# Attention and router stage of a gated block: who turns the attention outputs to token rows, and who normalises

## The chip, the cores and the metric

One core of a Trainium2 chip. The time is device microseconds of one execution; three runs of the kernel before gave 2321.11 us as their median (2320.79 to 2324.24). Inputs and outputs are float32.

## What is computed

```python
# x: (64, 128, 512), ctx: (64, 128, 128); 32 query heads on 8 key/value heads, head size 16
def xattn(q, k, v):
    scores = einsum('bkgsd,bktd->bkgst', qh, kh) / sqrt(16)
    weights = softmax(scores, axis=-1)
    return einsum('bkgst,bktd->bkgsd', weights, vh)      # back to (B, S, 512)

x = x + tanh(g_xattn) * xattn(layernorm(x), ctx, ctx)
h = layernorm(x)                                          # 8192 rows of 512
probs = softmax(h @ Wr)                                   # 32 experts, top 4, renormalised
shared = (silu(h @ Wsg) * (h @ Wsu)) @ Wsd * sigmoid(h @ Wse)
# each expert takes its first 64 (row, choice) pairs through silu(.Wg) * (.Wu) @ Wd
x = x + tanh(g_ffn) * (shared + weighted expert outputs)
```

## The kernel before

The program has two stages. The first is the attention stage, one loop over the 64 batches of 128 rows; it also adds the residual, computes the second normalisation and the router's logits, and picks the top four experts. The second stage runs the shared and the routed experts, in tiles of 512 rows; the change does not touch it. Everything below is about the first stage.

Each engine runs its own hand-written program, and the engines meet only at semaphores. `iterations` calls `body(B)` for B = 0 to 67, the middle ones in a hardware loop of two bodies a turn. So the order of an engine's work is the order of its `body`, and the work is pipelined by hand: in one body an engine works on several batches. A body has four chunks, c = 0 to 3. In the notation of the code, b = B - 2 means that the step is for the batch two before.

What TensorE does in a body, by name and line: p_exp, the scores of batch B - 1 (L663), one chunk each; in every chunk four transpositions of the next query chunk into p_tq (`q_cols`, L622) and the score maxima of batch B into p_max (L711); `k_cols` of batch B + 1 in chunk 3 (L614), into the bank p_pv; `pv`, the product of the exponentials with the values, in chunk 0 for (B - 2, half 1) and in chunk 2 for (B - 1, half 0) (L638), into p_pv; `o_cols`, which turns the evacuated product to token rows in p_ot (L648), in chunks 1 and 3; the transposition of the normalised x of B - 3 in chunk 1 (L673), into p_pv; the router's logits of B - 4 in chunk 2 (L686), into p_ot; and p_mt, the transposed maxima, in chunks 0 and 2 (L699). p_max, p_tq, p_pv, p_ot and p_mt each have one buffer: the next user waits until the last one has been read.

VectorE reduces p_max in every chunk (L561), normalises x for the queries (`norm_x`, L504), takes the statistics of x (L489, `bn_stats`, and L495), inverts the sums and normalises the outputs out of p_ot (L517, L527), adds the residual (L540), takes the statistics of the sum, normalises it (L504 again, target xn), and runs the router's selection (L546 copy of the logits, L573, L580, L585, L597). ScalarE does the exponentials (L439), and evacuates p_tq (L423), p_pv (L416, L417 for the keys, L428 for the outputs, L452 for the transposed x) and p_mt (L446). GpSimd splits keys and queries into their stacks (L339 to L342, L358, L362), computes one over the deviation (`inverse_root`, L327 and L331), books the selection (`take_top`) and splits a part of the shared weights (L400). SP issues the DMAs.

`pv` puts four groups into four quarters of p_pv's partitions, 512 columns each (four heads by 128 rows), so that what is evacuated has head dimensions on the partitions and has to be turned:

```python
for q in range(4):
    g = 4 * s + q
    last = mm(p_pv[32 * q:32 * q + 32, :], vals[b.par][:, g, :],
              probs[2 * s + q // 2][:, 512 * (q % 2):512 * (q % 2) + 512], start=True, stop=True)
```

Of the kernel before, what the change touches and what calls it, by code (L numbers as in the profile page):

```python
# [98 lines left out]
def build(nc, x, ctx_in, g_xattn, g_ffn, Wr, Wg, Wu, Wd, Wsg, Wsu, Wsd, Wse, out):  # L99
# [7 lines left out]
    with stack:  # L107
# [29 lines left out]
        with ExitStack() as scope:  # L137
# [11 lines left out]
            ot_sb = [sb(f"ot_sb{i}", [128, 512]) for i in range(2)]  # L149
# [19 lines left out]
            is_top = [sb(f"is_top{i}", [128, TOPK, NE]) for i in range(2)]  # L169
            two_sum = sb("two_sum", [128, 2, NE])  # L170
# [32 lines left out]
            pv_mm, ot_mm, mt_mm = sem("pv_mm"), sem("ot_mm"), sem("mt_mm")  # L203
# [36 lines left out]
            def _(sp):  # L240
# [12 lines left out]
                def body(B):  # L253
# [4 lines left out]
                    for c in range(NC):  # L258
# [6 lines left out]
                        if c == 0:  # L265
# [41 lines left out]
            def _(pool):  # L307
# [15 lines left out]
                def inverse_root(b, stat, mv, ve, rs, used, done):  # L323
# [7 lines left out]
                    nc.gpsimd.tensor_tensor(rs[:, :], ve[:, :], mhalf[:, :], ALU.pow).then_inc(done, 1)  # L331
# [50 lines left out]
                def body(B):  # L382
                    if isinstance(B.n, int) and B.n == 0:
                        inverse_root(B, stat1, mv1, ve1, rs1, qraw_done, rs1_done)
                        k_stacks(B)
                        q_stacks(B)
                        inverse_root(B + 1, stat1, mv1, ve1, rs1, qraw_done, rs1_done)
# [3 lines left out]
                    if (B - 5).ok:  # L391
                        take_top(B - 5)
                    if (B + 2).ok:
                        inverse_root(B + 2, stat1, mv1, ve1, rs1, qraw_done, rs1_done)
                    if (B - 2).ok:
                        inverse_root(B - 2, stat2, mv2, ve2, rs2, xn_done, rs2_done)
# [823 lines left out]
```

## Time and profile before

| | |
|---|---|
| median of 3 runs | 2321.11 us |
| the profiled execution, its own time | 2320.78 us |
| its span, first to last instruction | 2319.0 us |
| mean granted TensorE clock | 0.996 of full speed |
| TensorE busy | 2281.3 us (98%) |
| VectorE busy | 1154.4 us (50%) |
| ScalarE busy | 763.7 us (33%) |
| GpSimd busy | 594.0 us (26%) |
| DMA | 235.11 MB, mean 101 GB/s |

The shares are over the whole span, and the two stages differ: in the first, up to about 727 us, four engines work side by side; in the second TensorE leads. In what follows PE is TensorE's matmul stream, PEld its weight loads, which may run ahead of the matmuls, DVE is VectorE, ACT is ScalarE, POOL is GpSimd. A busy PE says little by itself, because the ends of pipelined matmuls are modelled; how far apart the groups start says more.

### The profile page before, as it was taken

How to read it: one execution, taken by the hardware profiler on the slowest of the kernel's cores; microseconds unless marked ns; L12 is line 12 of the kernel's file. 1: busy time of each engine (PE TensorE's matmuls, PEld its weight loads, DVE VectorE, ACT ScalarE, POOL GpSimd, SP SyncE). 2: the span in 40 equal slices, each digit the busy share in tenths (PEclk: the TensorE clock that was granted, in tenths of full speed). 3: DMA queues.
4: the chain of work that ended last, by engine and by line, in shares of the span. 5: the costliest groups of instructions: out<-in, count | busy, mean ns of one | idle time of the engine just before them, and what ended most of it. 6: DMA issues, size and time to landing. Idle time of an engine off the chain costs nothing.

```text
span 2319.0 us, 40286 instructions
## 1 busy us (share of the span) xinstructions
PE 2281.3 (98%) x12417; PEld 1760.4 (76%) x12417; DVE 1154.4 (50%) x2218; ACT 763.7 (33%) x1312; POOL 594.0 (26%) x1395
## 2 busy tenths in 40 slices
PE   6999999999997999999999999999999999999999
PEld 4777777777776877777777777778777777777777
DVE  6999999999996733222232322233232332323232
ACT  5888888888884111010100101011010110101010
POOL 5677777777763100000000000000000000000100
PEclk9999999999998999999999999999999999999999
DMA  3555555555554132322122222222222123222421
GB/s 85 142 142 145 144 144 141 145 145 144 138 153 137 19 119 88 114 84 81 63 79 84 97 86 82 79 68 97 99 84 79 63 81 119 81 83 75 137 67 43
DMA packets 269453, 235.11 MB, mean 101 GB/s; under 512 B 120545, under 2 KB 196321, under 8 KB 269410
## 3 DMA queue, kind: packets, MB, share of 16 engines
q1 hardware_dynamic: 265058, 221.89, 31.9%
q0 software_dynamic: 4352, 12.65, 1.9%
q8 instruction: 26, 0.43, 0.1%
q14 instruction: 17, 0.14, 0.0%
HBM read 161.88 MB, written 71.57 MB: 101 GB/s over the span
## 4 chain that ended last, share of the span: by engine, by line
PE 67%; DVE 1%; DMA 0%; issue 0%; DVEq 0%; POOLq 0%
PE acc L1126 7%; PE p_u L1142 7%; PE p_u L1144 7%; PE p_u L1143 7%; PE acc L1128 7%; PE acc L1127 7%; PE p_g L1142 7%; PE p_g L1144 7%; PE p_g L1143 7%; PE p_x L1174 2%; PE p_y L1161 2%; PE p_x L1161 2%; PE p_x L1152 0%; DMA rows<-out_dram 0%; PE p_y L1167 0%; DVE rows L1106 0%
## 5 line engine op out<-in xcount | busy, mean ns | idle before, releaser
L1060 DVE TENSOR_TENSOR act_f<-p_u,act_f 128x512 f32<-128x512 f32 x176 | 121.8, 692 | 982.7 <-PE p_u L1144 982.6
L965 ACT ACTIVATE act_f<-p_g 128x512 f32<-128x512 f32 x176 | 105.3, 598 | 1215.8 <-PE p_g L1144 1194.8
L561 DVE TENSOR_REDUCE negmax<-p_max 128x8 f32<-128x1024 f32 x256 | 312.8, 1222 | 49.6 <-PE p_max L711 47.8
L1126 PE MATMUL acc<-wd_h,hh 128*128 128x512 f32 x704 | 279.5, 397 | 0.0
L1142 PE MATMUL p_u<-xh,wgu_h 128*128 128x512 f32 x704 | 274.1, 389 | 4.0 <-DVE act_f L1060 4.0
L1142 PE MATMUL p_g<-xh,wgu_h 128*128 128x512 f32 x704 | 275.6, 391 | 0.0
L1127 PE MATMUL acc<-wd_l,hh 128*128 128x512 f32 x704 | 274.3, 390 | 0.0
L1128 PE MATMUL acc<-wd_h,hl 128*128 128x512 f32 x704 | 274.3, 390 | 0.0
L1144 PE MATMUL p_g<-xh,wgu_l 128*128 128x512 f32 x704 | 274.0, 389 | 0.0
L1144 PE MATMUL p_u<-xh,wgu_l 128*128 128x512 f32 x704 | 273.9, 389 | 0.0
L1143 PE MATMUL p_u<-xl,wgu_h 128*128 128x512 f32 x704 | 273.9, 389 | 0.0
L1143 PE MATMUL p_g<-xl,wgu_h 128*128 128x512 f32 x704 | 273.9, 389 | 0.0
L439 ACT ACTIVATE probs<-p_exp 128x1024 f32<-128x1024 f32 x256 | 261.2, 1020 | 31.8 <-PE p_exp L663 27.8
L711 PE MATMUL p_max<-kt,qt 128*128 128x256 f32 x1024 | 185.2, 303 | 1.5 <-DVE negmax L561 1.4
L1126 PEld LDWEIGHTS acc<-wd_h,hh 128*128 128x128 f32 x704 | 132.1, 188 | 47.6 <-DVE hl L1066 13.0
L663 PE MATMUL p_exp<-qt,kt 128*128 128x512 f32 x512 | 163.5, 401 | 0.2
L922 POOL DMA_INDIRECT eo<-out_dram,cur_tok x32 | 31.2, 976 | 505.0 <-DMA out_dram<-rows 408.3
L622 PE MATMUL p_tq<-ident,qs 128*128 128x128 f32 x1024 | 155.8, 275 | 2.6 <-POOL qs L362 1.8
L1142 PEld LDWEIGHTS p_u<-xh,wgu_h 128*128 128x128 f32 x704 | 132.2, 188 | 32.3 <-DVE act_f L1060 4.9
L1128 PEld LDWEIGHTS acc<-wd_h,hl 128*128 128x128 f32 x704 | 132.2, 188 | 28.0
L1144 PEld LDWEIGHTS p_g<-xh,wgu_l 128*128 128x128 f32 x704 | 132.2, 188 | 27.6
L1144 PEld LDWEIGHTS p_u<-xh,wgu_l 128*128 128x128 f32 x704 | 132.2, 188 | 27.4
(142 smaller groups left out, 3545.2 us busy)
## 6 DMA issues: line engine op xcount, KB each, us to landing
ew<-in_L_ffn_Wg_dram SPq DMA_DIRECT2D x32, 704.0 KB, 6.0
ew<-in_L_ffn_Wu_dram SPq DMA_DIRECT2D x32, 704.0 KB, 7.4
xs<-in_x_dram SPq DMA_DIRECT2D x64, 256.0 KB, 2.6
xres<-in_x_dram SPq DMA_DIRECT2D x64, 256.0 KB, 2.9
out_dram<-x SPq DMA_DIRECT2D x64, 256.0 KB, 2.7
xn_rows<-xn SPq DMA_DIRECT2D x64, 256.0 KB, 3.0
xn_cols<-xnT SPq DMA_DIRECT2D x64, 256.0 KB, 3.3
rows<-out_dram SPq DMA_DIRECT2D x16, 1024.0 KB, 5.2
```

The source lines that it names most:

```text
L439: nc.scalar.activation(probs[c][:, :], p_exp[:, :, :].rearrange("p a b -> p (a b)"), ACT.Exp, scale=float(D) ** -0.5).then_inc(exp_done, 1)
L561: nc.vector.tensor_reduce(negmax[c // 2][:, :].rearrange("p (g c i) -> p c i g", g=2, c=2)[:, c % 2, :, :], p_max[:, :, :].rearrange("p a ...
L622: last = tr(p_tq[:, 128 * i:128 * i + 128], qs[b.par][:, c, i, :, :].rearrange("p g r -> p (g r)"), ident[:, :])
L663: last = mm(p_exp[:, g2, :], kt[b.par][:, c, 128 * g2:128 * g2 + 128], qt[b.par][:, c, :], start=True, stop=True)
L711: last = mm(p_max[:, i // 2, 256 * (i % 2):256 * (i % 2) + 256], qt[B.par][:, c, 128 * i:128 * i + 128], kt[B.par][:, c, :], start=True, s ...
L1060: nc.vector.tensor_tensor(act_f[:, :], p_u[:, :], act_f[:, :], ALU.mult).then_inc(h_done, 1)
L1126: mm(acc[:, j, :], a[:, t], wd_h[:, f, :], start=(f == 0), stop=False)
L1127: mm(acc[:, j, :], a[:, t], wd_l[:, f, :], start=False, stop=False)
L1128: last = mm(acc[:, j, :], b[:, t], wd_h[:, f, :], start=False, stop=(f == FC - 1))
L1142: mm(bank[:, :], wgu_h[:, w, k, cols], xh[:, k, :], start=(k == 0), stop=False)
L1143: mm(bank[:, :], wgu_h[:, w, k, cols], xl[:, k, :], start=False, stop=False)
L1144: last = mm(bank[:, :], wgu_l[:, w, k, cols], xh[:, k, :], start=False, stop=(k == KC - 1))
```

## The change

- `pv` writes the product in 16 pieces, one for each of four groups of heads and four blocks of 32 rows: the 32 rows' block chooses the partition quarter, the group the columns. Each piece has 128 columns (four heads by 32 rows).
- With this layout a transposition of 32x32 blocks gives token rows. VectorE does it, out of p_pv into SBUF (`turn`, tile `turned`). TensorE's `o_cols` and ScalarE's `pv_evac` are gone. Reciprocal and normalisation of the outputs read `turned`.
- Both normalisations go from VectorE to ScalarE, as one Identity with scale and bias; GpSimd's `inverse_root` computes the bias nm = -mean * rs besides, with one more instruction.
- xn's transposition goes into p_ot. The logits go to chunk 3, their copy to ScalarE, and the selection follows one batch later (B - 5, `take_top` B - 6).
- SP stores xn at the end of the body.

```diff
@@ SP @@
-                            if (B - 3).ok:
-                                b = B - 3
-                                wait(sp, xn_done, b.n + 1)
-                                sp.dma_start(xn_dram[bass.ts(b.n, 128), 0:E], xn[b.par][:, :]).then_inc(xn_out[b.par], 16)
...
+                    if (B - 3).ok:
+                        b = B - 3
+                        wait(sp, xn_done, b.n + 1)
+                        sp.dma_start(xn_dram[bass.ts(b.n, 128), 0:E], xn[b.par][:, :]).then_inc(xn_out[b.par], 16)
@@ GpSimd, inverse_root @@
-                    nc.gpsimd.tensor_tensor(rs[:, :], ve[:, :], mhalf[:, :], ALU.pow).then_inc(done, 1)
+                    chain.inc(nc.gpsimd.tensor_tensor(rs[:, :], ve[:, :], mhalf[:, :], ALU.pow))
+                    chain.wait(pool)
+                    alone(pool, spare_p)
+                    nc.gpsimd.tensor_scalar(nm[:, :], mv[b.par][:, 0:1], rs[:, 0:1], -1.0, ALU.mult, ALU.mult).then_inc(done, 1)
@@ ScalarE @@
-                def pv_evac(b, s):
-                    act.wait_ge(pv_mm, 2 * b.n + s + 1)
-                    wait(act, ot_mm, 2 * (b.n - 1) + s + 1)
-                    nc.scalar.activation(ot_sb[s][:, :], p_pv[:, :], ACT.Copy).then_inc(pv_done, 1)
+                def norm_x(b):
+                    act.wait_ge(rs1_done, b.n + 1)
+                    wait(act, qs_done, b.n - 1)
+                    nc.scalar.activation(qraw[b.par][:, :], xs[b.par][:, :], ACT.Identity, bias=nm1[:, 0:1], scale=rs1[:, 0:1]).then_inc(qraw_done, 1)
+
+                def norm_x2(b):
+                    act.wait_ge(rs2_done, b.n + 1)
+                    wait(act, xnT_mm, b.n - 1)
+                    wait(act, xn_out[b.par], 16 * b.half)
+                    nc.scalar.activation(xn[b.par][:, :], x2[b.par][:, :], ACT.Identity, bias=nm2[:, 0:1], scale=rs2[:, 0:1]).then_inc(xn_done, 1)
...
+                        if c == 0 and (B + 1).ok:
+                            norm_x(B + 1)
...
-                        if c == 0 and (B - 2).ok:
-                            pv_evac(B - 2, 1)
-                        if c == 2 and (B - 1).ok:
-                            pv_evac(B - 1, 0)
+                        if c == 0 and (B - 3).ok:
+                            norm_x2(B - 3)
...
+                        if c == 3 and (B - 4).ok:
+                            b = B - 4
+                            act.wait_ge(lg_mm, b.n + 1)
+                            wait(act, kept, b.n - 1)
+                            nc.scalar.activation(lg[b.par][:, :], p_ot[:, 0:NE + 1], ACT.Copy).then_inc(lg_done, 1)
@@ VectorE @@
+                def turn(b, s):
+
+                    dve.wait_ge(pv_mm, 2 * b.n + s + 1)
+                    wait(dve, ot_done, 2 * (b.n - 1) + s + 1)
+                    nc.vector.transpose(turned[s][:, :, :].rearrange("p n r -> p (n r)"), p_pv[:, :]).then_inc(pv_done, 1)
@@ TensorE @@
                     for q in range(4):
-                        g = 4 * s + q
-                        last = mm(p_pv[32 * q:32 * q + 32, :], vals[b.par][:, g, :],
-                                  probs[2 * s + q // 2][:, 512 * (q % 2):512 * (q % 2) + 512], start=True, stop=True)
+                        heads = probs[2 * s + q // 2][:, 512 * (q % 2):512 * (q % 2) + 512].rearrange("p (i s) -> p i s", i=G)
+                        for j in range(4):
+                            last = mm(p_pv[32 * j:32 * j + 32, 128 * q:128 * q + 128], vals[b.par][:, 4 * s + q, :],
+                                      heads[:, :, 32 * j:32 * j + 32], start=True, stop=True)
                     last.then_inc(pv_mm, 1)
-
-                def o_cols(b, s):
-                    pe.wait_ge(pv_done, 2 * b.n + s + 1)
...
```

What waits for the bank p_pv keeps its line in `k_cols`: `wait(pe, pv_done, 2 * b.n - 3)`, for batch B + 1 the count that was reached by the evacuation of (B - 1, half 0) and is now reached by its `turn`.

The rest of the change is the order. TensorE before, chunks 2 and 3 of one body (p_tq<-ident,qs are q_cols, p_pv<-ident,ks k_cols, p_ot<-wr,xnT the logits):

```order
L663 MATMUL p_exp<-qt,kt 128x512 x2
L638 MATMUL p_pv<-probs,vals 32x512 x4
L686 MATMUL p_ot<-wr,xnT 128x33 x4
L699 MATMUL p_mt<-ident,negmax 16x128
L622 MATMUL p_tq<-ident,qs 128x128 x4
L711 MATMUL p_max<-kt,qt 128x256 x4
L663 MATMUL p_exp<-qt,kt 128x512 x2
L614 MATMUL p_pv<-ident,ks 128x128 x4
L648 MATMUL p_ot<-ident,ot_sb 128x128 x4
L622 MATMUL p_tq<-ident,qs 128x128 x4
L711 MATMUL p_max<-kt,qt 128x256 x4
```

The same place of the change:

```order
L676 MATMUL p_exp<-qt,kt 128x512 x2
L660 MATMUL p_pv<-probs,vals 32x128 x16
L707 MATMUL p_mt<-ident,negmax 16x128
L645 MATMUL p_tq<-ident,qs 128x128 x4
L719 MATMUL p_max<-kt,qt 128x256 x4
L676 MATMUL p_exp<-qt,kt 128x512 x2
L637 MATMUL p_pv<-ident,ks 128x128 x4
L698 MATMUL p_ot<-wr,xnT 128x33 x4
L645 MATMUL p_tq<-ident,qs 128x128 x4
L719 MATMUL p_max<-kt,qt 128x256 x4
```

The logits have moved from behind PV to behind k_cols, and o_cols is gone from there.

VectorE before, from the reduction of chunk 1 to that of chunk 3:

```order
L561 TENSOR_REDUCE negmax<-p_max 128x4x2
L540 SCALAR_TENSOR_TENSOR x_0<-o_sb,tanh_x,xres 128x512
L546 COPY lg<-p_ot 128x33
L489 BN_STATS st<-x_0 128x6
L561 TENSOR_REDUCE negmax<-p_max 128x4x2
L573 MAX v_0<-lg 128x8
L495 BN_AGGR mv_0<-st 128x2
L580 MAX_INDEX i<-v_0,lg 128x8
L561 TENSOR_REDUCE negmax<-p_max 128x4x2
```

The same place of the change, with what follows to the end of the body:

```order
L610 TENSOR_REDUCE negmax<-p_max 128x4x2
L594 SCALAR_TENSOR_TENSOR x_0<-o_sb,tanh_x,xres 128x512
L506 BN_STATS st<-x_0 128x6
L523 STREAM_TRANSPOSE turned<-p_pv 128x512
L561 CAST idx_f<-i 128x4
L512 BN_AGGR mv_0<-st 128x2
L610 TENSOR_REDUCE negmax<-p_max 128x4x2
L568 TENSOR_TENSOR is_top<-iota_e,idx_f 128x128
L610 TENSOR_REDUCE negmax<-p_max 128x4x2
L529 RECIPROCAL rec<-turned 128x16
L539 TENSOR_TENSOR o_sb<-turned,rec 128x256
```

The turn of (B - 1, half 0) stands between the statistics of x2 and the reduction of chunk 2, the selection's cast and the aggregation have moved ahead of that reduction. In chunk 0 the turn of (B - 2, half 1) stands ahead of the reduction, and the statistics of x, max8, reciprocal, aggregation, max_index and normalise stand between the reductions of chunks 0 and 1.

## Rows read from the trace of the kernel before

**Rows 1.** Busy time by engine (--windows), 400 to 700 us; first row names the columns.

```profile
core 0: us, PE busy (x) PEld busy (x) DVE busy (x) ACT busy (x) POOL busy (x), PEclk, DMA share, GB/s
400.00:700.00 300.00, 299.30 (x2282) 219.59 (x2281) 280.31 (x581) 254.37 (x431) 210.78 (x537) 1.00 0.54 146
```

**Rows 2.** Groups of instructions in 400:700: busy us, mean ns, then idle us before.

```profile
L561 DVE TENSOR_REDUCE negmax<-p_max 128x8 f32<-128x1024 f32 x112 | 136.9, 1222 | 15.5 <-PE p_max L711 14.6
...
L504 DVE TENSOR_SCALAR xn<-x,mv,rs 128x512 f32<-128x512 f32 x28 | 21.6, 770 | 0.0
...
L504 DVE TENSOR_SCALAR qraw<-xs,mv,rs 128x512 f32<-128x512 f32 x27 | 14.5, 536 | 0.0
...
L546 DVE COPY lg<-p_ot 128x33 f32<-128x33 f32 x27 | 4.9, 181 | 0.9 <-PE p_ot L686 0.9
```

**Rows 3.** Timeline of VectorE, one batch: start us, us, instruction, idle before.

```profile
502.83 0.68 DVE L489 BATCH_NORM_STATS2 st<-xs 128x6 f32<-128x512 f32 x1
...
503.43 0.23 DVE L517 RECIPROCAL rec<-p_ot 128x16 f32<-128x16 f32 x1
503.66 0.18 DVE L495 BATCH_NORM_AGGREGATE mv<-st 128x2 f32<-128x6 f32 x1
...
503.77 0.42 DVE L527 TENSOR_TENSOR o_sb<-p_ot,rec 128x256 f32<-128x256 f32 x1
...
504.11 1.22 DVE L561 TENSOR_REDUCE negmax<-p_max 128x8 f32<-128x1024 f32 x1
...
505.24 0.90 DVE L540 SCALAR_TENSOR_TENSOR x<-o_sb,tanh_x,xres 128x512 f32<-128x512 f32 x1
...
506.18 0.69 DVE L489 BATCH_NORM_STATS2 st<-x 128x6 f32<-128x512 f32 x1
...
508.07 0.18 DVE L573 MAX8 v<-lg 128x8 f32<-128x32 f32 x1
...
508.18 0.17 DVE L495 BATCH_NORM_AGGREGATE mv<-st 128x2 f32<-128x6 f32 x1
...
508.48 0.18 DVE L580 FIND_INDEX8 i<-v,lg 128x8 uint32<-128x32 f32 x1
...
509.10 1.23 DVE L561 TENSOR_REDUCE negmax<-p_max 128x8 f32<-128x1024 f32 x1 [0.43 <-PE p_max L711]
...
514.77 1.22 DVE L561 TENSOR_REDUCE negmax<-p_max 128x8 f32<-128x1024 f32 x1
```

**Rows 4.** Timeline of VectorE, the reduction of chunk 1 sixteen batches later.

```profile
676.63 1.22 DVE L561 TENSOR_REDUCE negmax<-p_max 128x8 f32<-128x1024 f32 x1
```

**Rows 5.** Timeline of TensorE and of ScalarE's evacuation, the same batch.

```profile
500.49 0.57 ACT L428 ACTIVATE ot_sb<-p_pv 128x512 f32<-128x512 f32 x1
...
501.25 0.42 PEld L673 LDWEIGHTS p_pv<-ident,xn 128*128 128x128 f32 x4 [0.33 <-ACT ot_sb L428]
...
503.71 0.16 PEld L638 LDWEIGHTS p_pv<-probs,vals 128*32 128x32 f32 x8 [0.36 <-issue]
503.71 1.07 PE L638 MATMUL p_pv<-probs,vals 128*32 128x512 f32 x8
...
504.71 1.08 PE L686 MATMUL p_ot<-wr,xnT 128*128 128x33 f32 x8
...
505.62 0.27 PE L699 MATMUL p_mt<-ident,negmax 128*16 128x128 f32 x1
...
507.11 0.60 PE L614 MATMUL p_pv<-ident,ks 128*128 128x128 f32 x4
...
507.55 0.60 PE L648 MATMUL p_ot<-ident,ot_sb 128*128 128x128 f32 x4
...
507.88 0.47 PEld L622 LDWEIGHTS p_tq<-ident,qs 128*128 128x128 f32 x4
```

**Rows 6.** Groups of instructions, whole span: 512 elements out of PSUM, and ScalarE out of SBUF.

```profile
L1060 DVE TENSOR_TENSOR act_f<-p_u,act_f 128x512 f32<-128x512 f32 x176 | 121.8, 692 | 982.7 <-PE p_u L1144 982.6
...
L946 ACT ACTIVATE xh<-chosen 128x512 fp32r<-128x512 f32 x60 | 33.0, 621 | 32.7 <-PE p_u L1144 32.7
```

More of the change, by code:

```diff
@@ L148, in build @@
             probs = [sb(f"probs{i}", [128, 2 * 512]) for i in range(4)]
-            ot_sb = [sb(f"ot_sb{i}", [128, 512]) for i in range(2)]
+            turned = [sb(f"turned{i}", [128, 16, 32]) for i in range(2)]
             o_sb = sb("o_sb", [128, E])
@@ L451, in body @@
                             wait(act, lg_mm, b.n - 1)
[L452 to L456 removed]
+                            nc.scalar.activation(xnT[b.par][:, :, :].rearrange("p k t -> p (k t)"), p_ot[:, :], ACT.Copy).then_inc(xnT_done, 1)
+                        if c == 0 and (B - 3).ok:
+                            norm_x2(B - 3)
                         if c == 3 and (B + 1).ok:
@@ L531, in body @@
                         aggregate(B, st1, stats_x(B), mv1, stat1)
-                        norm_x(B)
                         aggregate(B + 1, st1, stats_x(B + 1), mv1, stat1)
                     for c in range(NC):
+                        if c == 0 and (B - 2).ok:
+                            turn(B - 2, 1)
+                        if c == 1:
+                            if (B - 2).ok:
+                                inverted = invert_sums(B - 2, 1)
+                            if (B + 2).ok:
+                                wait(dve, rs1_done, B.n + 1)
+                                aggregate(B + 2, st1, x_stats, mv1, stat1)
+                            if (B - 5).ok:
+                                top_count = top_places(B - 5, top_count)
+                            if (B - 2).ok:
+                                normalise(B - 2, 1, inverted)
                         if c == 2 and (B - 2).ok:
@@ L575, in body @@
[L575 to L586 removed]
+                            if (B - 5).ok:
+                                top_count = top_eight(B - 5)
@@ L669, in body @@
                             pe.wait_ge(xn_done, b.n + 1)
-                            pe.wait_ge(pv_done, 2 * b.n + (4 if (b + 1).ok else 2))
-                            wait(pe, xnT_done, b.n)
+                            wait(pe, lg_done, b.n - 1)
                             for k in range(KC):
-                                last = tr(p_pv[:, 128 * k:128 * k + 128], xn[b.par][:, 128 * k:128 * k + 128], ident[:, :])
+                                last = tr(p_ot[:, 128 * k:128 * k + 128], xn[b.par][:, 128 * k:128 * k + 128], ident[:, :])
                             last.then_inc(xnT_mm, 1)
@@ L678, in body @@
                             pv(B - 1, 0)
-                        if c == 2 and (B - 4).ok:
+                        if c == 3 and (B - 4).ok:
                             b = B - 4
-                            pe.wait_ge(xnT_done, b.n + 1)
-                            pe.wait_ge(ot_done, 2 * b.n + 6 if (b + 2).ok else 2 * NB)
-                            wait(pe, lg_done, b.n)
+                            pe.wait_ge(xnT_done, b.n + (2 if (b + 1).ok else 1))
+                            if not (b + 1).ok:
+                                pe.wait_ge(lg_done, b.n)
                             for k in range(KC):
@@ L689, in body @@
                             pv(B - 2, 1)
-                        if c == 1 and (B - 2).ok:
-                            o_cols(B - 2, 1)
-                        if c == 3 and (B - 1).ok:
-                            o_cols(B - 1, 0)
                         b, h = (B - 1, 1) if c == 0 else (B, 0)
```

130 lines of the change are left out of this document (54 added, 76 removed).

## The prediction

> **What bounds the kernel now.** I read the windows first. In 400 to 700 us, inside the attention loop, TensorE is busy 299.3 of 300 us, VectorE 280.3, ScalarE 254.4, GpSimd 210.8 [rows 1]. The same reduction L561, 16 batches apart, starts at 504.11 and 676.63 [rows 3, 4]: 10.78 us a batch. The batch that I read closely takes 10.66 (its neighbour, with the loop's branch, some 0.2 more). Per batch that is VectorE 10.0 us, ScalarE 9.0, GpSimd 7.5. TensorE and VectorE are both nearly without gaps: in the timeline VectorE's instructions follow each other from 502.83 to 508.6, and its only real idle time is 0.43 us ahead of the reduction at 509.10 [rows 3]. So an average tells little; what counts is the order in which the two engines hand p_max and p_pv to each other. All that the change touches lies in this loop (up to about 727 us); the expert stage behind it is the same code.
>
> **Terms.**
>
> *TensorE loses o_cols.* Four transpositions take 0.44 us (7.11 to 7.55 in rows 5), eight of them 0.88 us a batch. The xn transposition moves from p_pv to p_ot and costs the same; the logits move from chunk 2 to chunk 3, 0.91 us either way [rows 5].
>
> *PV is cut into 16 products of 128 columns.* Before, eight passes of 512 columns, four side by side, take 1.07 us, and the next group starts 1.00 us after the first [rows 5]. The columns streamed are the same. Lower bound: the same 1.00 us. Upper bound: nothing runs side by side, 32 passes at the 0.11 us of a transposition, 3.5 us. I take 1.0 to 1.2, because the four neighbours still write four different partition quarters, as now, and their eight weight loads are issued within 0.16 us [rows 5].
> The Trainium skill ("TensorE: Matmul & The Clock Gate", Part 1) gives a floor of about 25 ns between starts of matmuls, or 62 ns where the sequencer decodes them. By the first, 32 passes would be 0.8 us and change nothing; by the second 2.0 us. The row above shows eight loads far closer together than either, but only as a burst.
>
> *VectorE.* Gone are norm_x (0.54), norm_x2 (0.77) and the lg copy (0.18) [rows 2]. New are two block transpositions of 128x512 from PSUM. No row shows one. Nearest is L1060, 512 elements from PSUM in 0.69 us [rows 6]. Lower bound 0.54, a 512-element instruction of the cheapest kind (norm_x); upper bound 1.22, as if it went over the data twice (the 1,024-element reduction). I take 0.69. Reciprocal and normalise now read SBUF; they cost what they cost now or up to 0.06 less each. Net: -1.49 + 1.38, less 0 to 0.24. VectorE's load stays within 0.4 us of the 10.0.
>
> *ScalarE* swaps two evacuations for two normalisations (a 512-column ACTIVATE out of SBUF is 0.62, L946 [rows 6]; the evacuation at 500.49 is 0.57 [rows 5]) and gets the lg copy: 9.0 to about 9.4 us, below the period. *GpSimd* gets two small instructions a batch with a wait ahead of each, under 1 us on 7.5. Its wait for qraw gets shorter, since ScalarE normalises ahead of the first exp and not behind VectorE's reduction. *SP:* the store of xn goes behind the loads and the out store of its batch; its reader comes two batches later, so nothing. If ScalarE or GpSimd were late, k_stacks or qraw would be late next; both have over half a batch.
>
> *Where the turn now stands.* This is the term that decides. p_pv has one bank, and three users in turn: PV, k_cols, and (before) xn. k_cols of the next batch waits in chunk 3 for the bank to be read. Before, ScalarE read it right after PV. Now VectorE's turn(B-1, 0) must, and it stands behind the reduction of chunk 1, x2 and the statistics of x2 (the order rows above show it). Behind k_cols on TensorE now stand the logits, q_cols and p_max of chunk 3, for whose reduction VectorE then waits. Following that loop from reduction 1 to reduction 1, start to start:
> - reduction 1.13 (4.11 to 5.24); x2 0.84 mean and 0.04 until statistics may start, 0.88; statistics 0.60 (2.83 to 3.43) [rows 3];
> - turn 0.69, and 0.19 until TensorE's first weight load (ACT L428 ends at 501.06, PEld L673 starts 501.25 [rows 5]); so far 3.49;
> - k_cols 0.44, logits 0.91, q_cols and p_max until the reduction starts 1.22 (weight load 507.88 to 509.10) [rows 3, 5]; 6.06;
> - reduction 3 in full 1.22 and 0.19; p_mt 0.11; q_cols and p_max 1.22; 8.80;
> - reduction 0 1.13, statistics 0.60, max8 0.11, reciprocal 0.23, aggregate 0.11, max_index 0.20, normalise 0.34 [rows 3]; 11.52.
>
> **11.5 us against the 10.66 of the same batch**, while either engine alone would need about 10. On the path are therefore the turn and the logits; off it are o_cols, PV (0.2 us of room in chunk 0) and all of ScalarE's. I take +0.8 a batch on 58 full batches (of 64, less the first and last that lack the router or the output step): +46 us. The end of the loop gets one router step later and two longer links (nm, ScalarE's norm): +2. The profiled execution took 2320.8 us (span 2319.0), 0.3 below the median, which changes nothing: **2369 us**.
>
> Its own range: turn at 0.54 and the four small instructions 0.06 cheaper give 11.1, +24, 2345; turn at 1.22 gives 12.05, +78, 2399.
>
> **Rivals.**
>
> *A. The work decides, and it gets faster.* If the turn came early enough, TensorE would need 10.66 - 0.88 + 0 to 0.2 = 9.8 to 10.0 and VectorE 9.6 to 9.9; at 10.0 the loop saves 0.7 x 60 = 42: 2279. For it speaks that both engines run nearly gapless now, so the loops they form have found room. It decides from the point where turn(B-1, 0) ends before TensorE is through p_exp of chunk 3, that is some 0.5 us earlier, and the rest of the loop is also 0.4 shorter. Against it: the order is written out and VectorE is strictly in order, and even without the wait of k_cols the path by reduction 2 is 1.13 + 0.88 + 0.60 + 0.61 + 0.18 + 1.41 + 0.79 = 5.60 instead of 6.06, 11.06 in all. This is the other sign.
> The Trainium skill ("VectorE: DVE Perf Modes", The three transpose paths) has a 128x128 bf16 transposition at 311 ns on VectorE against 390 on TensorE and calls VectorE's the fastest within a 32x32 block; by that rule the move gains. No row here shows that form, and the loop above is against it: TensorE's cost is 0.11 us each in a stream, not its latency.
>
> *B. No change.* It needs the loop at 10.7: nothing that I can name gives 0.8 back except sums of small errors (releases faster than 0.19, twice; cheaper small instructions). 2321.
>
> *C. The block transposition takes twice,* 1.22: 2399, or a little over.
>
> *D. PV costs more.* Between the bounds, at 2.0 us (32 passes at a bit over half the pace of a transposition [rows 5], side by side in part only), 0.2 of the extra 1.0 is covered in chunk 0, so +0.8 more a batch: 2415. At 3.5 us TensorE alone needs about 15 a batch: some 2580. For it: the passes are four times as many, and a quarter as long. Against it: they stay in four quarters.
>
> **Numbers.** Forecast 0.60; A 0.15; B 0.04; C 0.10; D 0.08 and 0.02 in its extreme; 0.01 for a faster case in between. Slower: 0.80; same 0.04; faster 0.16 (over or under 0.2%, about 5 us, is what a measurement of this kernel can tell from no change). Range 2335 to 2400: my own case, its cheap end with 10 us of doubt on the count, and most of C. Left out are A, B and D.
>
> **What would show it.** In the profile after: a STREAM_TRANSPOSE of about 0.7 us; L561's fellow at 11.4 to 11.6 us a batch; weight loads of k_cols (p_pv<-ident,ks) that wait 0.4 to 0.7 us for VectorE's turn in each batch; the p_max of chunk 3 later than now, with VectorE idle 0.5 us ahead of its reduction; TensorE's busy share in 400:700 near 90%. PV's 32 passes near 1.1 us. A turn over 1 us makes it C; PV over 1.5 us D. I am wrong if k_cols does not wait, or if the period is under 10.8 with all that in place.

## The result, and the profile after

The changed kernel takes **2347.77 us** (median of 4 runs, 2346.22 to 2349.66) beside 2321.92 (2320.79 to 2324.24) of the kernel before: a ratio of 1.011, 95% interval 1.0093 to 1.0128. It is slower by 26 us. I had said 2369 and 2335 to 2400: right in direction and inside the range, and about twice too much. The profiled execution has a span of 2347.8 us against 2319.0.

Windows of the changed kernel, 400 to 700 us, to set beside [rows 1]:

```profile
core 0: us, PE busy (x) PEld busy (x) DVE busy (x) ACT busy (x) POOL busy (x), PEclk, DMA share, GB/s
400.00:700.00 300.00, 275.11 (x3248) 219.66 (x3248) 264.76 (x533) 259.85 (x442) 222.71 (x569) 1.00 0.51 137
```

TensorE and VectorE both got gaps: 299.3 has become 275.1, 280.3 has become 264.8. Per batch VectorE's busy time went from 10.07 us (280.3 x 10.78 / 300) to 9.92 (264.8 x 11.24 / 300) and TensorE's from 10.75 to 10.31. The work fell on both, and the loop still got longer. Groups of VectorE and ScalarE in the same stretch, beside [rows 2]:

```profile
L610 DVE TENSOR_REDUCE negmax<-p_max 128x8 f32<-128x1024 f32 x108 | 131.2, 1214 | 32.4 <-PE p_max L719 32.1
L523 DVE STREAM_TRANSPOSE turned<-p_pv 128x512 f32<-128x512 f32 x54 | 37.8, 701 | 0.0
L539 DVE TENSOR_TENSOR o_sb<-turned,rec 128x256 f32<-128x256 f32 x53 | 27.4, 517 | 0.9
...
L433 ACT ACTIVATE qraw<-xs,nm,rs 128x512 f32<-128x512 f32 x27 | 22.0, 814 | 0.0
L439 ACT ACTIVATE xn<-x,nm,rs 128x512 f32<-128x512 f32 x27 | 21.6, 799 | 0.0
```

The turn is 0.70 us. VectorE now waits 32.1 us in 300 for p_max, where it waited 14.6. The list of waits (engine and line, what it waited for: us in total, times, longest) has what I looked for first:

```profile
DVE negmax L610 <- PE p_max L719: 32.1, 40, 1.1
...
PEld p_pv L637 <- DVE turned L523: 19.1, 27, 0.8
```

In each of the 27 batches the weight loads of k_cols wait 0.7 us for VectorE's turn. One round of VectorE, from reduction 1 to reduction 1, and the same reduction 16 batches later (timeline: start, us, instruction, idle before):

```profile
500.24 1.21 DVE L610 TENSOR_REDUCE negmax<-p_max 128x8 f32<-128x1024 f32 x1
501.37 0.75 DVE L594 SCALAR_TENSOR_TENSOR x<-o_sb,tanh_x,xres 128x512 f32<-128x512 f32 x1
502.15 0.69 DVE L506 BATCH_NORM_STATS2 st<-x 128x6 f32<-128x512 f32 x1
502.76 0.70 DVE L523 STREAM_TRANSPOSE turned<-p_pv 128x512 f32<-128x512 f32 x1
...
503.51 1.19 DVE L610 TENSOR_REDUCE negmax<-p_max 128x8 f32<-128x1024 f32 x1
...
505.97 1.23 DVE L610 TENSOR_REDUCE negmax<-p_max 128x8 f32<-128x1024 f32 x1 [1.07 <-PE p_max L719]
...
508.71 1.23 DVE L610 TENSOR_REDUCE negmax<-p_max 128x8 f32<-128x1024 f32 x1 [0.25 <-PE p_max L719]
...
511.42 1.22 DVE L610 TENSOR_REDUCE negmax<-p_max 128x8 f32<-128x1024 f32 x1
...
680.11 1.21 DVE L610 TENSOR_REDUCE negmax<-p_max 128x8 f32<-128x1024 f32 x1
```

(680.11 - 500.24) / 16 = 11.24 us a batch; before it was 10.78 [rows 3, 4]. 0.46 x 60 = 27 us, all of the loss. The last reduction of the loop starts at 703.2 before and at 730.7 after, 27.5 later. From there to the end it is 1615.8 us before and 1617.1 after, so the experts' stage costs what it did to within the spread of the runs.

The most useful table is that of the steps from each reduction to the next (start to start, us, from the timelines; each batch has one of each):

| | 0 to 1 | 1 to 2 | 2 to 3 | 3 to 0 | batch, mean of 48 |
|---|---|---|---|---|---|
| before, one body | 2.87 | 2.81 | 2.16 | 2.80 | 10.78 |
| before, mean | 2.86 | 2.84 | 2.16 | 2.91 | 10.78 |
| after, one body | 2.71 | 3.27 | 2.46 | 2.74 | 11.24 |
| after, mean | 2.77 | 3.27 | 2.46 | 2.74 | 11.24 |

(The loop has two bodies; the other one is up to 0.25 longer in one step. Steps given below are of one body unless they are called means.) Before, VectorE has at most 0.17 us of gap ahead of its reductions in 3 to 0, 0 to 1 and 1 to 2, and only 2 to 3 is a hand-over by way of TensorE. In the means, the change took 0.17 out of 3 to 0 and 0.09 out of 0 to 1, and it put the turn into 1 to 2, which was already full and grew by 0.43; from there the turn pushes k_cols, and 2 to 3 grew by 0.29.

The same batch on TensorE:

```profile
503.51 0.42 PEld L637 LDWEIGHTS p_pv<-ident,ks 128*128 128x128 f32 x4 [0.66 <-DVE turned L523]
...
503.90 0.97 PEld L698 LDWEIGHTS p_ot<-wr,xnT 128*128 128x128 f32 x8
...
504.71 0.50 PEld L645 LDWEIGHTS p_tq<-ident,qs 128*128 128x128 f32 x4
...
506.33 0.81 PEld L660 LDWEIGHTS p_pv<-probs,vals 128*32 128x32 f32 x32 [0.36 <-issue]
...
507.34 0.09 PEld L707 LDWEIGHTS p_mt<-ident,negmax 128*16 128x16 f32 x1 [0.20 <-issue]
```

The turn ends at 503.46 and k_cols starts at 503.51; the logits and Q follow without a gap. PV in 32 passes takes 1.01 us to the next group, as it did in 8.

### The profile page after: what moved, and what is told of

Its sections match the earlier page's. It is cut to its first block, busy times and chain, and to the rows that moved or that the text cites. A ratio compares the mean times of both kernels' runs of the same rounds, so it can differ in the third digit from the quotient of the medians.

```text
span 2347.8 us, 45660 instructions
## 1 busy us (share of the span) xinstructions
PE 2255.0 (96%) x14977; PEld 1783.5 (76%) x14977; DVE 1141.5 (49%) x2154; ACT 802.1 (34%) x1376; POOL 637.0 (27%) x1523
## 4 chain that ended last, share of the span: by engine, by line
PE 66%; DVE 1%; DMA 0%; issue 0%; DVEq 0%; POOLq 0%
PE acc L1134 7%; PE p_u L1150 7%; PE p_u L1152 7%; PE p_u L1151 7%; PE acc L1135 7%; PE acc L1136 7%; PE p_g L1150 7%; PE p_g L1152 7%; PE p_g L1151 7%; PE p_x L1182 2%; PE p_y L1169 2%; PE p_x L1169 2%; PE p_x L1160 0%; DMA rows<-out_dram 0%; PE p_y L1175 0%; DVE rows L1114 0%
## 5 line engine op out<-in xcount | busy, mean ns | idle before, releaser
L453 ACT ACTIVATE probs<-p_exp 128x1024 f32<-128x1024 f32 x256 | 261.4, 1021 | 32.8 <-PE p_exp L676 32.1
L645 PE MATMUL p_tq<-ident,qs 128*128 128x128 f32 x1024 | 162.8, 282 | 2.6 <-POOL qs L366 1.9
L428 ACT ACTIVATE qt<-p_tq 128x512 fp32r<-128x512 f32 x256 | 150.7, 589 | 19.6 <-PE p_tq L645 12.1
```

The lines of the kernel that those rows point to most:

```text
L428: nc.scalar.activation(qt[b.par][:, c, :], p_tq[:, :], ACT.Copy).then_inc(tq_done, 1)
L453: nc.scalar.activation(probs[c][:, :], p_exp[:, :, :].rearrange("p a b -> p (a b)"), ACT.Exp, scale=float(D) ** -0.5).then_inc(exp_done, 1)
L645: last = tr(p_tq[:, 128 * i:128 * i + 128], qs[b.par][:, c, i, :, :].rearrange("p g r -> p (g r)"), ident[:, :])
```

## Experiments

Twelve kernels ran. Each is an edit of the changed kernel, unless it says otherwise; the ratio is to the kernel before, run beside it. "Batch" is the mean of the same 48 batches.

### e1_turn_before_stats

```diff
-                            dve.wait_ge(x2_done, b.n + 1)
-                            x2_stats = stats(x2[b.par][:, :], st2)
                         if c == 2 and (B - 1).ok:
                             turn(B - 1, 0)
+                        if c == 2 and (B - 2).ok:
+                            dve.wait_ge(x2_done, (B - 2).n + 1)
+                            x2_stats = stats(x2[(B - 2).par][:, :], st2)
```

> The change with one edit: VectorE's turn of (B - 1, half 0) ahead of the statistics of x2, not behind them. Theory (the turn's place): in the change the turn ends at 503.46 and k_cols starts at 503.51, 0.61 after p_exp of chunk 3 is through (about 502.90); then logits, q_cols and p_max stand behind it. Now the turn starts 0.61 earlier, k_cols no longer waits for it, q_cols ends at 504.57, and p_max of chunk 3 starts when reduction 2 ends (504.70), 0.43 earlier than now (505.18): 10.8 us a batch for 11.24, so 0.43 x 60 = 26 us less, 2322 us. Rival 1 (chunk 2 of VectorE is too full, whatever the turn's place: reduction 2 is what p_max of chunk 3 waits for): no change, 2348, since reduction 2 starts no earlier. Rival 2 (ScalarE's normalisations, at 0.80 us each and not 0.62, are on the path): no change, 2348.

Measured: 2339.06 (2337.49 to 2342.14), ratio 1.0078, 1.0061 to 1.0095; batch 11.09. Steps 2.71, 3.42, 2.12, 2.7 to 2.9. Timeline of VectorE:

```profile
505.33 1.22 DVE L611 TENSOR_REDUCE negmax<-p_max 128x8 f32<-128x1024 f32 x1
506.47 0.74 DVE L594 SCALAR_TENSOR_TENSOR x<-o_sb,tanh_x,xres 128x512 f32<-128x512 f32 x1
507.13 0.71 DVE L523 STREAM_TRANSPOSE turned<-p_pv 128x512 f32<-128x512 f32 x1
507.76 0.65 DVE L506 BATCH_NORM_STATS2 st<-x 128x6 f32<-128x512 f32 x1
508.33 0.15 DVE L561 CAST idx_f<-i 128x4 f32<-128x4 uint32 x1
508.56 0.18 DVE L512 BATCH_NORM_AGGREGATE mv<-st 128x2 f32<-128x6 f32 x1
508.75 1.23 DVE L611 TENSOR_REDUCE negmax<-p_max 128x8 f32<-128x1024 f32 x1
...
510.87 1.23 DVE L611 TENSOR_REDUCE negmax<-p_max 128x8 f32<-128x1024 f32 x1 [0.69 <-PE p_max L720]
```

The half that my theory is about came true: k_cols waits no longer (0.05 us where it was 0.71), and 2 to 3 falls from 2.46 to 2.12, a bare hand-over. But 1 to 2 grew by 0.15, and the whole gave 9 us of the 26 that I had expected. The turn no longer covers the time between the statistics and their aggregation: the aggregation starts 0.80 us after the statistics do, where the turn used to stand between them and only 0.04 us lay between the cast and the aggregation. The chunk is full of VectorE's own work in either order. Of the 0.46 us a batch that the change lost, the reordering gives back 0.15; the other 0.31 is still lost with k_cols free of the turn.

### e2_logits_chunk2

```diff
-                        if c == 3 and (B - 4).ok:
+                        if c == 2 and (B - 4).ok:
```

(TensorE's logits, back to where they stood before.)

> The change with one edit: TensorE's logits back in chunk 2, behind PV, as before the change. Theory: the turn still ends at 503.46, and k_cols waits for it; behind k_cols only q_cols is left (0.47), so p_max of chunk 3 comes at about 504.92 instead of 505.18 (reduction 2, itself 0.15 later because of the logits in chunk 2, ends at 504.87): 0.27 a batch, 16 us, 2332 us. Rival 1 (VectorE's chunk 2 decides): slower or the same, 2348 to 2357, as reduction 2 only comes later. Rival 2 (ScalarE): the same.

Measured: 2348.07 (2347.99 to 2349.66), ratio 1.0115, 1.0098 to 1.0131; batch 11.20. Steps 2.71, 3.4 to 3.6, 2.12, 2.85. A miss: 2 to 3 shrank by 0.34, and k_cols no longer waits for the turn (0.05 us), but in the means 1 to 2 grew by 0.21 and 3 to 0 by 0.11. In one body VectorE now waits 0.25 us for p_max of chunk 2, where it waited for nothing. So the logits cost as much in chunk 2 as in chunk 3, and taking the wait of k_cols away by itself gave nothing.

### e4_stats_behind and e7_router_behind_too

e4 moves x2's statistics, the cast and the aggregation behind reduction 2, and leaves x2, the turn and the mask ahead of their reductions:

```diff
-                            dve.wait_ge(x2_done, b.n + 1)
-                            x2_stats = stats(x2[b.par][:, :], st2)
...
-                            top_count = top_numbers(B - 5, top_count)
...
-                            aggregate(B - 2, st2, x2_stats, mv2, stat2)
...
                                                    AX.X, ALU.max, negate=True).then_inc(max_done, 1)
+                        if c == 2 and (B - 2).ok:
+                            dve.wait_ge(x2_done, (B - 2).n + 1)
+                            x2_stats = stats(x2[(B - 2).par][:, :], st2)
+                        if c == 2 and (B - 5).ok:
+                            top_count = top_numbers(B - 5, top_count)
+                        if c == 2 and (B - 2).ok:
+                            aggregate(B - 2, st2, x2_stats, mv2, stat2)
```

> The change with one more step than the first of these: VectorE's turn directly behind x2, and statistics of x2, cast and aggregation behind reduction 2, where VectorE waits 0.3 to 0.4 us for p_max now. Theory: k_cols starts at 502.90, reduction 2 at 502.82 (its p_max is ready then) for 503.51, so p_max of chunk 3 follows q_cols at 504.57: 0.61 a batch less, 10.6 us, 37 us in all, 2311 us; that beats the kernel before. Rival 1 (reduction 2 decides alone, not the turn): the same gain here, but none in the first. Rival 2 (ScalarE): the same as the change.

Measured: 2339.84 (2335.53 to 2340.68), ratio 1.0071, 1.0054 to 1.0087; batch 11.11, mean steps 2.98, 2.66, 2.58, 2.90. e7 moves max8 and max_index there too:

> As the one before, and max8 and max_index behind reduction 2 too (they stand between reductions 0 and 1 in the change, where VectorE is 0.65 us late for p_max). Theory: between reductions 0 and 1 they cost 0.38 of VectorE's time on the path, between 2 and 3 nearly nothing (0.05): another 0.33 a batch, 20 us: 10.3 us a batch, 2291 us. Rival (a work bound has been reached: VectorE 9.9 us plus the releases): no further gain, 2311.

Measured: 2339.89 (2337.24 to 2341.33), ratio 1.0076, 1.0059 to 1.0092; batch 11.13. Both missed, by 29 and 49 us, and the windows and one group of e4 say why (400 to 700 us):

```profile
400.00:700.00 300.00, 275.73 (x3296) 224.18 (x3295) 284.68 (x542) 259.05 (x446) 224.94 (x584) 1.00 0.52 139
```

```profile
L539 DVE TENSOR_TENSOR o_sb<-turned,rec 128x256 f32<-128x256 f32 x55 | 40.1, 729 | 1.0
```

VectorE's busy time rose to 284.68, that is 10.5 us a batch against 264.76 x 11.24 / 300 = 9.9 in the changed kernel, with the same instructions. The normalisation of the outputs has gone from 0.42 before the change and 0.52 after it to 0.73. VectorE and GpSimd, where it is worst:

```profile
510.40 0.94 POOL L404 TENSOR_TENSOR wgu_l<-wst,wgu_h 128x352 f32 x1
...
510.54 1.08 DVE L539 TENSOR_TENSOR o_sb<-turned,rec 128x256 f32<-128x256 f32 x1
```

In the changed kernel's own 53 normalisations the length goes by GpSimd's instruction beside it: 404 to 408 ns beside L380, 436 to 445 beside L362, 526 to 542 beside L366, 672 to 685 beside L404. The times of the ends say more: in the other 40 of the 53, GpSimd's instruction had started first, and VectorE's product ended 0.27 to 0.28 us after it; beside L380 VectorE had started first, and nothing was added. In the pair shown above GpSimd ends at 511.34 and VectorE at 511.62. All this is still a correlation; e17 below tests it.

### e16_half_turn

```diff
-                    nc.vector.transpose(turned[s][:, :, :].rearrange("p n r -> p (n r)"), p_pv[:, :]).then_inc(pv_done, 1)
+                    nc.vector.transpose(turned[s][:, 0:8, :].rearrange("p n r -> p (n r)"), p_pv[:, 0:256]).then_inc(pv_done, 1)
```

(Ahead of the loop both buffers of `turned` are filled with ones. Half of the attention outputs are left out.)

> The changed kernel with each turn cut to half its columns (128x256 in place of 128x512), so that half of the attention outputs are left out and everything else stays as it is. Theory (the turn of half 0 lies between reduction 1 and the K transposes, all of it on the path to reduction 3; the turn of half 1 lies beside TensorE's work before reduction 0): the turn takes about 0.36 in place of 0.70 us, reduction 1 to reduction 3 takes 5.40 in place of 5.74, reduction 3 to 0 keeps 2.73, a batch is 0.34 shorter, and the time is about 2348 - 60 x 0.34 = 2327. Rival 1 (the time is set by the sum of VectorE's work): both turns count, 0.68 a batch, 2307. Rival 2 (another engine or a wait elsewhere sets the batch): 2345 to 2348.

Measured: 2336.77 (2335.13 to 2337.97), ratio 1.0066, 1.0049 to 1.0083; batch 11.09. Groups of VectorE:

```profile
L541 DVE TENSOR_TENSOR o_sb<-turned,rec 128x256 f32<-128x256 f32 x55 | 34.3, 623 | 1.0
L525 DVE STREAM_TRANSPOSE turned<-p_pv 128x256 f32<-128x256 f32 x54 | 23.5, 435 | 0.0
```

Half the columns save 0.27 us, not 0.34 (0.435 against 0.701), and 1 to 2 falls by just that, from 3.27 to 3.00; 2 to 3 and 3 to 0 stay at 2.46 and 2.74. So what was cut from the turn of half 0 counts in full, and what was cut from that of half 1 not at all. But 0 to 1 grew from 2.77 to 2.89 in the mean, and the normalisation that stands in it from 0.47 to 0.58 us, because it fell beside other instructions of GpSimd. Hence 0.16 a batch: 11 us under the changed kernel, not 21.

### e5_norms_as_copies

```diff
-                    nc.scalar.activation(qraw[b.par][:, :], xs[b.par][:, :], ACT.Identity, bias=nm1[:, 0:1], scale=rs1[:, 0:1]).then_inc(qraw_done, 1)
+                    nc.scalar.activation(qraw[b.par][:, :], xs[b.par][:, :], ACT.Copy).then_inc(qraw_done, 1)
...
```

(The same for xn with nm2 and rs2. Both normalisations are left out.)

> The changed kernel with ScalarE's two normalisations as plain copies without scale and bias, which leaves the normalisation of x and of x2 out. It asks what their 0.81 and 0.80 us are made of and whether ScalarE is on the path. Theory (ScalarE has slack, and the two operands per partition are what makes them longer than the 0.6 us of ScalarE's other 128x512 copies): the two take 0.6 to 0.65 and the time stays within 3 us of the changed kernel's, 2345 to 2350. Rival (ScalarE's work holds up the Q copies and through them the path): 0.35 to 0.4 a batch less, 2324 to 2327. If the two still take 0.8 us, the operands are not the cause.

Measured: 2348.66 (2347.06 to 2351.25), ratio 1.0117, 1.0101 to 1.0134; batch 11.24. ScalarE's two groups:

```profile
L433 ACT ACTIVATE qraw<-xs 128x512 f32<-128x512 f32 x27 | 17.1, 632 | 0.0
L439 ACT ACTIVATE xn<-x 128x512 f32<-128x512 f32 x27 | 16.6, 614 | 0.0
```

The operands per partition cost 0.18 us each time, and taking 0.37 us a batch off ScalarE moves nothing: it is off the path.

### e8_norms_alone

The kernel before, with only the two normalisations put on ScalarE as in the change, and what goes with them: GpSimd's product for the bias, and the store of xn at the end of SP's body.

> The kernel before with only the two normalisations moved to ScalarE (and GpSimd's extra product for the bias); TensorE still transposes the outputs back. VectorE loses some 0.9 us a batch, ScalarE gains 1.6 on 9.14 busy, together 10.7 of 10.78. Theory: ScalarE becomes the engine that sets the batch, 10.9 to 11.1 us a batch, 2330 to 2345. Rival (VectorE's relief counts and ScalarE has just room enough): faster, 2300 to 2315. Third: nothing, 2320 to 2325.

Measured: **2400.36** (2399.06 to 2400.67), ratio 1.0341, 1.0323 to 1.0358; batch 12.08, mean steps 3.53, 3.58, 2.16, 2.80. Slower than any theory had it, and not for the reason given: ScalarE is busy 260.46 of 300 us, not full. TensorE's waits for it, and one of them in the timeline:

```profile
PEld p_pv L678 <- ACT ot_sb L443: 28.5, 24, 1.2
...
PE p_pv L678 <- ACT xn L438: 18.8, 24, 0.8
```

```profile
506.19 0.57 ACT L443 ACTIVATE ot_sb<-p_pv 128x512 f32<-128x512 f32 x1
...
506.67 0.80 ACT L438 ACTIVATE xn<-x,nm,rs 128x512 f32<-128x512 f32 x1
...
507.69 0.42 PEld L678 LDWEIGHTS p_pv<-ident,xn 128*128 128x128 f32 x4 [1.20 <-ACT ot_sb L443]
```

The normalisation of x, 0.8 us, stands at the head of chunk 0 on ScalarE, ahead of the exponentials and of the evacuation of p_pv, which has one bank. The normalisation of x2 stands right behind that evacuation, and TensorE wants its result in the next chunk. The list puts the 1.2 us of waiting down to the evacuation, but that had ended at 506.76; xn ended at 507.47, and in all 24 cases the weight load starts 0.9 us after the evacuation and 0.2 us after xn. So it is mostly xn that TensorE waits for here, in the step from 0 to 1. That the place in ScalarE's queue is what the move costs is my reading of these waits: no run moved it, and why 1 to 2 grew from 2.84 to 3.58 as well I did not take apart.

### e14_after_q_first and e15_before_q_first

TensorE's Q transposes ahead of the maxima's transposition in chunks 0 and 2, so that they need not wait for the reduction. First in the changed kernel:

```diff
+                        if c < 3 and B.ok:
+                            q_cols(B, c + 1)
...
                             last = tr(p_mt[:, :], negmax[h][:, :], ident[:, :])
                             last.then_inc(mt_mm, 1)
-                        if c < 3 and B.ok:
-                            q_cols(B, c + 1)
...
```

> The changed kernel with TensorE's Q transposes put ahead of the transposition of the maxima in chunks 0 and 2, so that they don't wait for reductions 3 and 1. Theory: reduction 3 to 0 is a pure hand-over now (reduction 3, p_mt, Q transposes, p_max, 2.73 us), and VectorE has 2.48 us of work in it (reduction, reciprocal, normalise, turn); so it falls to about 2.48, while reduction 1 to 2 is VectorE's own work and stays at 3.27: 0.25 a batch, about 2333. Rival 1: reduction 3 to 0 is VectorE's anyway and nothing moves, 2348. Rival 2: the maxima come later to the second pass, and its waits take the gain back or more, 2345 to 2360.

Measured: 2348.70 (2348.28 to 2349.50), ratio 1.0120, 1.0103 to 1.0137; batch 11.25, every step as in the changed kernel. Timeline from reduction 3 to reduction 0:

```profile
504.54 1.23 DVE L610 TENSOR_REDUCE negmax<-p_max 128x8 f32<-128x1024 f32 x1 [1.07 <-PE p_max L719]
504.90 0.81 PEld L660 LDWEIGHTS p_pv<-probs,vals 128*32 128x32 f32 x32 [0.37 <-issue]
...
505.91 0.42 PEld L645 LDWEIGHTS p_tq<-ident,qs 128*128 128x128 f32 x4 [0.20 <-issue]
...
506.41 0.54 PEld L719 LDWEIGHTS p_max<-kt,qt 128*128 128x128 f32 x4
...
507.28 1.23 DVE L610 TENSOR_REDUCE negmax<-p_max 128x8 f32<-128x1024 f32 x1 [0.26 <-PE p_max L719]
```

It was not the pure hand-over that I took it for. Between the two p_max TensorE has p_exp, PV (1.01), Q (0.39) and the maxima of its own, in a row, and they take as long as the way by the reduction did. By this timeline two paths of some 2.74 us stood side by side, and one was cut. The control is the same edit in the kernel before:

> A control for e19_same_q_first: the kernel before with nothing but TensorE's Q transposes ahead of the maxima's in chunks 0 and 2. Theory (before the change VectorE works without a gap from reductions 3 to 0, 0 to 1 and 1 to 2, and only from 2 to 3 does the hand-over by way of TensorE set the time, where this order changes nothing): 2318 to 2324, no change. Rival (the order is a gain for either kernel, and e19's lead over e18 has nothing to do with where the turn and the statistics stand): 0.1 to 0.2 a batch, 2308 to 2316.

Measured: 2341.32 (2340.43 to 2343.20), ratio 1.0088, 1.0072 to 1.0105; batch 11.15: slower, which neither theory had. The list of waits:

```profile
ACT mt L446 <- PE p_mt L703: 49.6, 40, 1.6
...
PEld p_pv L614 <- ACT ot_sb L428: 10.7, 26, 0.4
PEld p_pv L673 <- ACT ot_sb L428: 10.2, 26, 0.5
```

ScalarE copies the maxima ahead of its evacuation of p_pv. A later p_mt holds that up (49.6 us of waiting, 31.5 before), and k_cols and xn wait for the bank, 0.4 us each time (k_cols waited 0.04 before). Step 2 to 3 grows from 2.16 to 2.36; 1 to 2 grows by up to 0.17 and 3 to 0 by about 0.1, whose share I did not take apart.

### e17_rec_psum

```diff
-            rec = sb("rec", [128, 16])
...
-            p_mt = ps("p_mt", [16, 128])
+            p_mt = p_ot[0:16, 0:128]
+            rec = ps("rec", [128, 16])
...
```

(TensorE gets four more waits, which order the users of the bank that p_mt now shares.)

> The changed kernel with the reciprocals of the sums in a PSUM bank, as the one edit on VectorE: the normalisation of the outputs (L539) then reads only one operand from SBUF. To have a bank free, the transposed maxima go to a corner of the bank of the router's products, with four waits that order them. Theory (the normalisation is slowed, 0.40 to 1.08 us, where GpSimd's products run at the same time and both its operands lie in SBUF): it takes a flat 0.40 to 0.45, and chunks 0 to 1, where VectorE is without a gap, lose up to 0.1 a batch; 2342 to 2348 in time. Rival (two SBUF operands have nothing to do with it): it stays at a mean of 0.52 with the same spread, and the time at 2348.

Measured: 2347.18 (2346.38 to 2347.44), ratio 1.0108, 1.0091 to 1.0125; batch 11.21. The normalisation's group:

```profile
L539 DVE TENSOR_TENSOR o_sb<-turned,rec 128x256 f32<-128x256 f32 x54 | 22.2, 411 | 0.9
```

All 54 now lie between 400 and 421 ns, whatever GpSimd does. So the length came from two operands in SBUF at a time when an earlier instruction of GpSimd ran. In the changed kernel this alone is worth next to nothing, as expected.

### e18_stats_mask_behind_rec and e19_same_q_first

e18 is e4 with e17's edit, and with the mask behind chunk 3's normalisation:

> e4_stats_behind (x2's statistics, their aggregation and the router's numbers behind reduction 2) with the reciprocals in PSUM as in e17_rec_psum, and the router's mask behind the normalisation of chunk 3. In e4 VectorE had no gap left, and its busy time had grown from 9.9 to 10.5 us a batch, by normalisations of 0.67 to 1.08. Theory (these were what ate the gain): VectorE is back at 9.8 to 10.0 busy, a batch takes 10.5 to 10.8, and the time is 2305 to 2322, at or under the kernel before. Rival (VectorE's hand-overs, not the normalisations, fill it): as e4, 2336 to 2342.

Measured: **2315.87** (2313.74 to 2317.96, 10 runs), ratio 0.9974, 0.9965 to 0.9984; batch 10.69. Steps 2.6 to 2.7, 2.61, 2.57, 2.7 to 2.9.

```profile
400.00:700.00 300.00, 286.75 (x3407) 230.71 (x3405) 280.39 (x563) 267.43 (x460) 218.45 (x590) 1.00 0.54 145
```

VectorE's busy time is 280.39 x 10.69 / 300 = 10.0 a batch, and the time is near the 2311 that I had expected of e4. The fall in VectorE's busy time is the normalisation's, 0.41 for 0.73. The two edits were not tried apart, so how much of the 24 us over e4 is the mask's place stays open; but of the 0.42 us a batch that e18 gained, 0.32 lie in the step from 0 to 1 (2.98 to 2.66 in the mean), where the mask stands in neither kernel and the normalisation fell from 0.70 to 0.40. Step 2 to 3, which the mask left, stayed at 2.58. e19 adds the order of e14:

> e18_stats_mask_behind_rec with TensorE's Q transposes ahead of the maxima's in chunks 0 and 2. In the changed kernel this alone gave nothing (2348.70): between reductions 3 and 0 TensorE had p_exp 0.5, PV 1.0, Q 0.4, maxima 0.1 and p_max 0.72 of its own in a row, as long as the chain by way of the reduction. Theory (reduction 1 to 2 can now be shortened, since VectorE's work is gone from it, and reduction 3 to 0 can't): 0.1 to 0.3 a batch under e18, 2290 to 2312. Rival (VectorE's or TensorE's work holds there too): as e18 within 3 us.

Measured: **2306.58** (2305.94 to 2307.14), ratio 0.9932, 0.9915 to 0.9949; batch 10.53, and it is 1 to 2 that fell, from 2.61 to 2.43 and 2.54. The same edit was worth nothing in e14 and cost 21 us in e15. In e14 VectorE's own work still filled that step, and in e15 an evacuation stands behind the maxima's copy on ScalarE; in e19 neither is so, and there it pays. Neither condition was tried alone. e19 is faster than both kernels.

## Why the prediction was right, and half the size

**The deciding term held.** "Where the turn now stands" named the loop, the wait of k_cols and the idle time ahead of reduction 3. The wait is there in every batch (0.7 us; I had said 0.4 to 0.7), and VectorE waits 1.07 us ahead of reduction 3 where I had said 0.5. e16 shows the turn of half 0 on the path: the 0.27 us cut from it count in full. TensorE's busy share is 92% (I had said near 90%), but the batch of 11.24 lies under the 11.4 to 11.6 that I had named. e1 takes the first wait away and leaves 0.70 of the second, and it gives back only a third of the loss. So the wait of k_cols was the smaller part; the larger is that VectorE's step from 1 to 2 has the turn in it and is full. The prediction had this path too, under rival A ("even without the wait of k_cols", 5.60 from reduction 1 to 3 and 11.06 in all), and e1 measured just that: 5.54 and 11.09.

**Sizes, term by term.** Steps 3 to 0 and 0 to 1 were predicted at 2.74 and 2.72, and measured at 2.74 and 2.71. The error is all in reduction 1 to 3: 6.06 predicted, 5.73 measured (500.24 to 505.97).
- x2 and the step to the statistics: 0.88, measured 0.78. Its mean was 0.84 before and is 0.74 now, for the same instruction. It has two inputs in SBUF too, and no run tests what lengthened it. But in the trace of before, 26 of 28 started while GpSimd was in an earlier instruction (L362), took 0.80 to 0.91 us and ended 0.55 us after it; the other two took 0.74.
- The release from VectorE to TensorE: 0.19, measured 0.05 (503.46 to 503.51). I had used the row of ScalarE's evacuation of p_pv. But 0.19 is no price of ScalarE: in e15 TensorE's loads waited 53 times for the same evacuation, and 52 of them started 0.05 us after it (one pair is shown below). In the row that I used TensorE had also waited for VectorE's xn, which ended at 501.02, only 0.04 ahead of the evacuation. How the two waits make 0.19 was not tested.

```profile
510.06 0.57 ACT L428 ACTIVATE ot_sb<-p_pv 128x512 f32<-128x512 f32 x1
510.68 0.42 PEld L614 LDWEIGHTS p_pv<-ident,ks 128*128 128x128 f32 x4 [0.41 <-ACT ot_sb L428]
```

- The sum so far: with the statistics and the turn as predicted to 0.01 each, k_cols starts 3.27 after the reduction, and not 3.49.
- k_cols 0.44, measured 0.39; logits 0.91, measured 0.81 (load to load: 503.90 to 504.71). Q and p_max 1.22, measured 1.26. Before, both were timed start to start in a full queue of matmuls.

That makes 11.18 for this batch in place of 11.52. The rest of the error is the comparison: I set the loop against the closely read batch of 10.66, where the mean was 10.78, though I had both numbers. Written out for a batch: 0.86 predicted (of which I took 0.8), less 0.34 for the terms, less 0.12 for the base, plus 0.06 because the other body of the changed kernel is slower too (mean 11.24): 0.46 measured. In time these are 52 - 20 - 7 + 4, about 28 us. The step that failed is the sum "11.52" by its terms of release, x2, k_cols and logits, and the base "10.66"; the path from reduction 1 by the turn to reduction 3 did not.

**Other terms.** The turn: 0.69 taken, 0.70 measured. PV: 1.0 to 1.2 taken, 1.01 measured; rival D is out. The passes start four at a time, 7 ns apart, and the four again every 109 ns. The Trainium skill ("TensorE: Matmul & The Clock Gate", Part 1) has 25 ns as the least distance of starts; the mean here is 26, but inside a group of four, which write four different partition quarters, it does not hold. Rival C is out with the turn. Rival B's "sums of small errors" did give 0.34 of 0.8 back, and not the rest. The end of the loop: +2 predicted; from the last reduction to the end the two profiled executions differ by 1.3 us, which is within the spread of the runs.

**ScalarE** I had at 0.62 a normalisation; it takes 0.80 and 0.81. The row I used was a copy without operands. ScalarE's load rose to 9.7 us a batch (259.85 x 11.24 / 300), not to 9.4. It cost nothing, as e5 shows. The rule was to be had: the Trainium skill ("ScalarE: Activation LUTs", What ACT_TABLE_LOAD costs) gives 186 ns + 0.833 ns an element and 93 ns for each operand by pointer, an estimate of 0.61 without and 0.80 with the two, as measured here.

**Normalising the outputs** I had as equal or 0.06 cheaper out of SBUF; it became 0.10 dearer in the mean, and up to 0.27 (404 to 685 ns), because the reciprocal lies in SBUF as well. On the path that was worth little here (e17), but it made e4, e7 and a part of e16 miss. The Trainium skill ("SBUF — State Buffer", Who interferes with whom) says that a VectorE instruction with two SBUF inputs contends with a GpSimd instruction that reads SBUF, and that the order of issue decides which of the two is held up. The trace agrees: where GpSimd's had started first (40 of 53 in the changed kernel, all 54 in e4), VectorE's ended 0.27 to 0.29 us after it; where VectorE's had started first (13), it took 0.40 to 0.41.

**Rival A** (the work decides, 2279) needed the turn 0.5 us earlier and the loop 0.4 shorter. e1 gave the first, e4 tried for the second, and e18 and e19 reached 2316 and 2307, with the reciprocals in PSUM besides. That is 15 us under the kernel before, where A had 42: there is room of that kind, and a third of it was reached.

**What stays open:** why e15's steps 1 to 2 and 3 to 0 grew too, why e8's step 1 to 2 did, what made the 0.19 of the row of release, and the mask's share in e18.

## What to carry to other kernels

Before moving work to another engine, write down for each step between hand-overs which engine is without a gap in it: what e16 cut from the same turn counted in full in one step and for nothing in another, and the same edit of order was worth -9, 0 or +21 us by the kernel that it met. Where two or three engines pass one buffer round, look at a move's place in the queue before the sum of busy times: both engines had lost work here and the loop grew by 0.46 us. And take the base for a loop from the mean over many turns, and a hand-over's price from a row in which the waiting engine had nothing else left to wait for.

## What the runs showed of the hardware that I had not expected

- VectorE's block transposition from PSUM to SBUF in float32: 0.70 us for 128x512, 0.435 for 128x256, so by an estimate from these two sizes 1.04 ns an element of a row on a base of 0.17 us.
- A VectorE product with both inputs in SBUF took 0.40 to 1.09 us for 128x256: it ended 0.27 to 0.29 us after an instruction of GpSimd that had started before it (94 cases in the changed kernel and e4). With one of the inputs in PSUM it took 0.39 to 0.43 (the kernel before and e17).
- A release reached TensorE's waiting weight load in 0.05 us, from VectorE (27 cases in the changed kernel) and from ScalarE (52 of 53 in e15).
- 32 matmul passes of 128 columns, four side by side, took 1.01 us to the next group, and 8 of 512 took 1.00.
